# Dense stage of a three-stage transformer kernel: both layer normalisations applied by ScalarE in place of VectorE

## What is computed

```python
# ao: output of the first attention's heads, y: its normalised input, x: the input
r   = y + ao @ Wf.T + bf                       # out = res + _lin(out, Wf, bf)
on  = (r - mean(r)) / sqrt(var(r) + EPS) * g2 + b2
x1  = x + (r + relu(on @ Wr1.T + br1) @ Wr2.T + br2)
x2  = x1 + ffn(_layernorm(x1))                 # _layernorm(x) = (x - m) / sqrt(v + eps)
```

## Time and profile before

| | us |
|---|---|
| median of 3 runs | 1937.64 |
| lowest, highest | 1916.83, 1940.32 |
| span of the profiled execution | 1922.6 |
| dense stage in it, first transfer issued to the next stage's first | 918.46 to 1135.44 |

### The profile page before, as it was taken

The page is one execution under the profiler, slowest core; times in us unless marked ns, Lnnn a source line. Parts: engine busy times, 40 slices in busy tenths (PEclk is TensorE's granted clock), DMA queues, the critical chain, the costliest instruction groups (busy, mean ns, idle before and its releaser), DMA issues. The chain is left out here.

```text
span 1922.6 us, 45960 instructions
## 1 busy us (share of the span) xinstructions
PE 1565.6 (81%) x13604; PEld 1346.2 (70%) x13668; DVE 1446.9 (75%) x3554; ACT 767.5 (40%) x1731; POOL 866.4 (45%) x1116
## 2 busy tenths in 40 slices
PE   5998988898888988887566645888888888888887
PEld 3988888888888888887355524666666666666665
DVE  5587878887788878876588855777778777777774
ACT  1555555555555555554122221333333333333331
POOL 4355555554555555554455542333343333333331
PEclk8999999999999999999699876999899888898896
DMA  4422122212222222210333212223222222222221
GB/s 122 133 98 77 63 71 82 74 64 74 74 77 71 71 76 74 76 66 21 109 94 99 82 52 77 91 95 100 96 91 96 88 87 88 87 93 87 89 86 37
DMA packets 178621, 158.08 MB, mean 82 GB/s; under 512 B 9457, under 2 KB 160113, under 8 KB 178546
## 3 DMA queue, kind: packets, MB, share of 16 engines
q1 hardware_dynamic: 178546, 157.16, 24.7%
HBM read 113.09 MB, written 44.04 MB: 82 GB/s over the span
## 5 line engine op out<-in xcount | busy, mean ns | idle before, releaser
L578 PE MATMUL a_bank<-a_vp,a_prob 128*128 128x96 f32 x4096 | 662.0, 268 | 0.0
L578 PEld LDWEIGHTS a_bank<-a_vp,a_prob 128*128 128x128 f32 x4096 | 638.4, 200 | 8.2
L666 DVE TENSOR_REDUCE a_nmax<-a_bank 128x2 f32<-128x512 f32 x512 | 347.2, 684 | 158.7 <-PE a_bank L547 157.4
L472 ACT ACTIVATE a_prob<-a_bank 128x512 f32<-128x512 f32 x512 | 306.0, 598 | 359.1 <-PE a_bank L562 358.2
L547 PE MATMUL a_bank<-a_k_st,a_q_st 96*128 96x256 bf16 x1024 | 272.3, 291 | 98.0 <-DMA a_k_st<-scratch_a_parts_dram 90.8
L562 PE MATMUL a_bank<-a_q_st,a_k_st 120*128 120x256 bf16 x1024 | 289.7, 283 | 2.7 <-POOL a_q_st L335 2.7
L335 POOL TENSOR_SCALAR a_q_st<-a_mt 24x2048 bf16<-24x2048 bf16 x64 | 121.4, 1896 | 245.2 <-PE a_bank L562 138.2
L1760 DVE TENSOR_REDUCE c_nmax<-c_bank 128x4 f32<-128x512 f32 x256 | 167.4, 684 | 53.2 <-PE c_bank L1572 51.7
L1602 PE MATMUL c_o_bank<-c_vb,c_prob 128*128 128x96 f32 x1024 | 182.3, 304 | 30.1 <-DVE c_ad L1885 29.2
L547 PEld LDWEIGHTS a_bank<-a_k_st,a_q_st 96*128 96x128 bf16 x1024 | 122.5, 124 | 113.9 <-issue 76.3
L1476 ACT ACTIVATE c_prob<-c_bank 128x256 f32<-128x256 f32 x256 | 98.8, 386 | 200.6 <-PE c_bank L1552 199.0
(11 more groups left out here) (200 smaller groups left out, 3059.6 us busy)
## 6 DMA issues: line engine op xcount, KB each, us to landing
a_q_st<-scratch_a_parts_dram SPq DMA_DIRECT2D x192, 96.0 KB
a_k_st<-scratch_a_parts_dram SPq DMA_DIRECT2D x64, 288.0 KB
c_q_st<-scratch_c_parts_dram SPq DMA_DIRECT2D x192, 96.0 KB
c_k_st<-scratch_c_parts_dram SPq DMA_DIRECT2D x64, 288.0 KB
scratch_a_parts_dram<-a_parts SPq DMA_DIRECT2D x32, 384.0 KB, 2.7
scratch_c_parts_dram<-c_parts SPq DMA_DIRECT2D x32, 384.0 KB, 2.7
a_x<-in_x SPq DMA_DIRECT2D x32, 128.0 KB, 11.3
scratch_y<-a_y SPq DMA_DIRECT2D x32, 128.0 KB, 10.8
```

The source lines that it names most:

```text
L472: act.activation(prob[h % 4][:, :, :].rearrange("p a b -> p (a b)"), t_ps[h % 2][:, :], ACT.Exp).then_inc(exped, 1)
L578: mm = pe.matmul(o_ps[g % 2][:, at:at + VC], prob[h % 4][:, c, t * P:(t + 1) * P], vp[o][:, c, :], start=c == 0, stop=c == NT - 1)
L666: dve.tensor_reduce(nmax[:, t, 2 * g:2 * g + 2], s_ps[t][:, :].rearrange("p (h k) -> p h k", h=2), AX.X, ALU.max, negate=True).then_inc(ma ...
```

## The change

ScalarE computes z = rs * r + shift with one Identity activation for each block of 128 columns, scale and bias being columns of rs and of the new tile `shift`. GpSimd makes two more short operations for each norm: negm = -mean and shift = negm * rs; a norm now counts four steps on its semaphore (NORM) where it counted two. On ScalarE, norm 1 of unit n-1 stands between the copy of A and `on`, and norm 2 of unit n-2 between the second relu and the copy of Z1. On VectorE all z are gone, so the moments of norm 1 follow r directly. The waits that guarded the buffers r and x1 against being written too early move to the two additions, and the moments wait for GpSimd's norm rather than for z.

```diff
--- before.py
+++ after.py
@@ -842,6 +842,7 @@
         z1, z1t, x2 = two("z1_", [P, C, P]), two("z1t", [P, C * P]), two("x2_", [P, C, P])
         stats, mv = two("stats", [P, C, 6]), two("mv", [P, C, 2])
         var, rs = two("var", [P, C]), two("rs", [P, C])
+        negm, shift = two("negm", [P, C]), two("shift", [P, C])
         bank = [ctx.enter_context(nc.psum_tensor(f"b_bank{i}", [P, 512], F32)) for i in range(8)]
         aot_ps, zt_ps, z1t_ps, r_ps, h_ps, f_ps, g_ps = *bank[0:4], bank[4:6], bank[6], bank[7]
 
@@ -867,7 +868,7 @@
         z1t_p, z1t_d = sem("z1t_p"), sem("z1t_d")
         g_p, x2_d, x2_out = sem("g_p"), sem("x2_d"), sem("x2_out")
 
-        N_LOAD, N_LATE = 4, 3
+        N_LOAD, N_LATE, NORM = 4, 3, 4
         units = lambda a: a.rearrange("b t f -> (b t) f").rearrange("(j u c p) f -> j u p c f", u=2, c=C, p=P)
         x_dram, y_dram, ao_dram, x2_dram = units(d["x"]), units(d["y"]), units(d["ao"]), units(d["x2"])
         wc_dram = d["folded"].rearrange("(j u) p f -> j u p f", u=2)
@@ -944,8 +945,12 @@
                 pool.wait_ge(mv_d[k], (n + 1) * C)
                 apart(pool, spare)
                 pool.tensor_scalar(var[k][:, :], mv[k][:, :, 1], EPS, 1.0, ALU.add, ALU.mult).then_inc(norm_d[k], 1)
-                pool.wait_ge(norm_d[k], 2 * n + 1)
+                pool.tensor_scalar(negm[k][:, :], mv[k][:, :, 0], -1.0, 1.0, ALU.mult, ALU.mult
+                                   ).then_inc(norm_d[k], 1)
+                pool.wait_ge(norm_d[k], NORM * n + 2)
                 pool.tensor_tensor(rs[k][:, :], var[k][:, :], half[:, :], ALU.pow).then_inc(norm_d[k], 1)
+                pool.wait_ge(norm_d[k], NORM * n + 3)
+                pool.tensor_tensor(shift[k][:, :], negm[k][:, :], rs[k][:, :], ALU.mult).then_inc(norm_d[k], 1)
 
             rows = lambda a: a[:, :].unsqueeze(1).broadcast_to([P, C, P])
 
@@ -987,6 +992,12 @@
         def _(act):
             act.wait_ge(loaded, N_LOAD * 16)
 
+            def normed(k, n, src, dst):
+                act.wait_ge(norm_d[k], NORM * (n + 1))
+                for c in range(C):
+                    act.activation(dst[:, c, :], src[:, c, :], ACT.Identity, scale=rs[k][:, c:c + 1],
+                                   bias=shift[k][:, c:c + 1]).then_inc(z_d[k], 1)
+
             def body(j, u):
                 n, i = 2 * j + u, u
                 if has(j, u, 0):
@@ -995,6 +1006,9 @@
                         act.wait_ge(r_p, n - 1)
                     act.copy(ao_t[i][:, :], aot_ps[:, :]).then_inc(aot_d, 1)
                 if has(j, u, 1):
+                    if later(j, n, 3):
+                        act.wait_ge(zt_p, n - 2)
+                    normed(0, n - 1, r[1 - i], z[1 - i])
                     act.wait_ge(zt_p, n)
                     if later(j, n, 3):
                         act.wait_ge(h_p, 2 * (n - 2))
@@ -1007,6 +1021,9 @@
                         act.activation(hid[1 - i][:, c, :], h_ps[c][:, :], ACT.Relu, bias=cols[:, c:c + 1]
                                        ).then_inc(hid_d, 1)
                 if has(j, u, 2):
+                    if later(j, n, 4):
+                        act.wait_ge(z1t_p, n - 3)
+                    normed(1, n - 2, x1[i], z1[i])
                     act.wait_ge(z1t_p, n - 1)
                     if later(j, n, 4):
                         act.wait_ge(g_p, n - 3)
@@ -1090,28 +1107,19 @@
                     apart(dve, spare)
                     dve.bn_aggr(mv[k][:, c, :], stats[k][:, c, :]).then_inc(mv_d[k], 1)
 
-            def normed(k, n, src, dst):
-                dve.wait_ge(norm_d[k], 2 * (n + 1))
-                for c in range(C):
-                    dve.tensor_scalar(dst[:, c, :], src[:, c, :], mv[k][:, c, 0:1], rs[k][:, c:c + 1],
-                                      ALU.subtract, ALU.mult).then_inc(z_d[k], 1)
-
             def body(j, u):
                 n, i = 2 * j + u, u
-                if has(j, u, 1):
-                    if later(j, n, 3):
-                        dve.wait_ge(zt_p, n - 2)
-                    normed(0, n - 1, r[1 - i], z[1 - i])
                 if has(j, u, 2):
 
                     dve.wait_ge(f_p, n - 1)
                     dve.wait_ge(xr_d, 2 * (n - 1))
                     if later(j, n, 4):
                         dve.wait_ge(xb_d, n - 3)
+                        dve.wait_ge(z_d[1], (n - 3) * C)
                     dve.tensor_tensor(flat(x1[i]), f_ps[:, :], flat(xr[i]), ALU.add).then_inc(x1_d, 1)
                     dve.wait_ge(x1_d, n - 1)
                     if later(j, n, 3):
-                        dve.wait_ge(z_d[1], (n - 2) * C)
+                        dve.wait_ge(norm_d[1], NORM * (n - 2))
                     moments(1, n - 2, x1[i])
                 if has(j, u, 3):
 
@@ -1126,15 +1134,11 @@
                     dve.wait_ge(yb_d, n + 1)
                     if later(j, n, 2):
                         dve.wait_ge(xr_d, 2 * (n - 1))
+                        dve.wait_ge(z_d[0], (n - 1) * C)
                     dve.tensor_tensor(flat(r[i]), r_ps[:, :], flat(yb[i]), ALU.add).then_inc(r_d, 1)
                     dve.wait_ge(r_d, n + 1)
                     if later(j, n, 1):
-                        dve.wait_ge(z_d[0], n * C)
-                if has(j, u, 2):
-                    if later(j, n, 4):
-                        dve.wait_ge(z1t_p, n - 3)
-                    normed(1, n - 2, x1[i], z1[i])
-                if has(j, u, 0):
+                        dve.wait_ge(norm_d[0], NORM * n)
                     moments(0, n, r[i])
 
             pipeline(dve, body, NU, 4, ahead=1)
```

## The result

| us | before | after |
|---|---|---|
| median (lowest to highest) | 1932.40 (1916.83 to 1941.82), 14 runs | 1909.37 (1898.00 to 1919.16), 14 runs |
| ratio after / before | | 0.9887, interval 0.9860 to 0.9915 |
| profiled execution: span | 1922.6 | 1905.7 (total 1907.45) |
| stage a / dense stage / last stage in it | 918.46 / 216.98 / 787.16 | 916.40 / 213.60 / 775.70 |

The prediction was 1932 (1914 to 1947), with -6 us for the change. Of the profiles' 16.9 us only 3.4 come from the dense stage, 2.1 from the first and 11.5 from the last (`attention_b`); no line of either was edited.

A forecast was written before the change was run, and what follows sets the result against it. VectorE was taken to bound the dense stage at 12.19 us per unit, afterwards a TensorE-ScalarE chain at 11.87; 13 units give 4.2 us and the ends 1.8, so -6.0 and a median of 1932 us, range 1914 to 1947.

The forecast's parts named there:

- The Sum: Dense stage: 13 units gain 4.2 us, the ends 1.8, together -6.0 us, taken off the whole kernel's span and median.
- The circle: Dense stage, one chain through TensorE, ScalarE and both norms: 11.05 us per unit at full clock, 12.68 at low, 11.87 taken.
- What it adds: Dense stage: ScalarE activations of 0.48 us, four in 1.59; GpSimd 0.6 us per norm, hidden by 2.6 and 3 us cover.
- Rival (c): Dense stage, ScalarE: activations with two pointers don't overlap, 1.92 us per norm; about 1942 us; chance 10%.
- (b): Dense stage, TensorE: the low clock strikes at every Z1 and F, 12.68 us per unit; about 1942 us; chance 12%.
- (e): Dense stage: ScalarE is the wrong engine, each z dearer than what it replaces on VectorE; 1944 us; chance 4%.
- The ends: First and last units of the dense stage: a gain of 1.8 us, bounds 0 and 4.
- Rival (d): Dense stage: freed VectorE hands the whole saving on, TensorE's 8.2 us become the period; -52 us, about 1885; chance 2%.
- Rival (a): Dense stage, TensorE: the clock stays high in nearly every unit, 11.05 us each; about 1921 us; chance 18%.

The follow-up runs named there:

- cut kernels: The kernel before and the changed kernel, each without its last stage, the dense stage writing the output: 1135.55 us and 1133.52 us.
- the early norm 2: The changed kernel with ScalarE's norm 2 moved behind `on` and ahead of both relus: 1869.11 us, ratio 0.9712, dense stage 175.3 us.
- the changed kernel with 20 increments: The changed kernel with 20 more idle semaphore increments on GpSimd behind the dense stage's code: 1923.58 us, ratio 1.0023; run again, 1926.27 us, ratio 0.9989.

## Why the prediction was wrong, step by step

- **"I read the dense stage alone, since the change touches nothing else."** This is the step that failed. The change also put 44 GpSimd instructions ahead of the last stage, and that moved the last stage by 8 to 17 us in the profiles of a job, while the dense stage gave 2.0 (cut kernels) to 3.4. The Sum then set the difference off against the whole kernel as if the other 1706 us were fixed, and the three times shown, 1.2% apart, were taken for noise without asking which stage makes it. The row that would have warned was in the trace of before: a subtraction of 0.28 us that takes 1.19 to 1.27 in 31 of its 64 places, each 0.02 to 0.11 us behind a start on GpSimd.
- **The circle was right.** Full-clock units in the middle 10.9 to 11.2 (said 11.05), low-clock ones 12.6 to 12.8 (12.68), slow F in 8 of 16 (half), which is as many as before. The eight units in the middle take 95.07 us, 11.88 each, where 11.87 stands in the prediction.
- **What it adds was right.** Activations of 0.481 (0.48), four in 1.65 (1.59; the step is 0.39 rather than 0.37); shift ready at 1004.89 and wanted at 1007.47, a cover of 2.6 us as said; the norm chain from var to its last product is 1.84 us where it was 1.29, 0.55 longer (0.6). The Trainium skill has this form's cost (ScalarE: Activation LUTs, What ACT_TABLE_LOAD costs): by an estimate from its constants, for 128 columns and two pointers, 479 ns and a step of 386; the trace agrees with 481 and 0.39. Rival (c) falls with the step of 0.39, (b) with the clock high in every second unit, and (e) with a dense stage that is shorter and not longer.
- **The ends were mis-sized.** -1.8 was the term, with bounds of -4 and 0, and they cost +1.5. From the first x1 to the last the profiles have fifteen units in 177.8 us before and 177.6 after: the middle twelve are 4.9 us shorter, but the first distance is 1.8 longer (13.86 for 12.02) and the last two are 2.8 longer together (11.34 and 10.57 for 11.10 and 8.02). In the last units of before four z took 1.97 us on VectorE, as only one of the four was long, where they took 2.91 to 3.03 in the steady rhythm; so ScalarE's 1.65 saves 0.3 there and not 1.3. That its two normalisations in a row are pure chain once TensorE's queue is nearly empty is argued and wasn't tried by itself. The start of the stage to its first x1 gives 3.0 back. With the ends at +1.5 and the middle at -4.9 the sum is -3.4, not -6.0.
- **Rival (d) was refused for the right reason,** as the early norm 2 shows: take the order away and the gain comes, 38 us of dense stage.
- **Rival (a)** misjudged the clock's part: going from 2.9 to 2.3 us of standstill left the low clock in every second unit, and only the version without that standstill lost it.

What stays open: what holds GpSimd up at the 836th instruction, and what starts and ends a row of slow blocks, which come with 31 long subtractions and, in one of two kernels, with none. The gain's cause is shown down to the placement; the way from the placement to the rows of slow blocks is not.

## What to carry to other kernels

When an edit adds instructions to an engine's program, ask of every later loop of that engine which of its operations start within 0.1 us of an operation of a neighbour that it slows down; such ties can be decided by where the code lies, and a gain or loss of 1% can be theirs. Before crediting a change, cut the kernel behind the changed stage, and pad the old kernel with as many idle instructions as the new one has more. And before moving work to another engine, try the order on the old one: here the moments ahead of z gave the stage 19 us and the move gave 3, until norm 2 was put ahead of the relus, and the two together gave 42.

## What was not expected of the hardware

- **A short stall at a fixed place of a loop.** GpSimd's gap is 184 ns, but at one instruction of the last stage's loop 247 to 259 in each pass, 63 to 75 ns more, and 473 to 478 the first time. It moves with the number of instructions ahead (0, 64 and 256 more: not in this gap; 44 more: in it), and stays at the 836th instruction of the program, or at the 1092nd. The Trainium skill (Runtime: NRT & Kernel Launch, Instruction fetch mechanics) tells of instruction memory that is refilled in blocks of 256 instructions at a cost that is mostly hidden. The distance of 256 between the two places agrees with the traces; that the stall is this refilling is inferred from the distance, and no trace shows it. That it can come back in every pass is what these traces add, and here it was worth 0.07 us on GpSimd and about 15 on the kernel.
- **The first of two neighbours holds up the second.** VectorE's 64x128 subtraction takes 0.28 us, and 1.27 if it starts 0.02 us after GpSimd's 1.15 us operation; GpSimd's takes 1.26 if it starts 0.04 us later. A matter of 0.06 us is worth 1 us to VectorE.
- **Blocks at the low clock come in rows.** In the kernel before, blocks of 23.9 us with about 7 us of low clock each followed one another, up to 7 in a row there and up to 14 in the changed kernel with 20 increments; with the standstill at 0.78 us in every second block such rows never formed in the six profiles of that pattern. Standstills of 1.76 us stand in the quick blocks of before too, so the length of the standstill alone doesn't decide.
